# A mixture-of-experts layer behind cross-attention: eight full expert tiles moved into the end of the attention part, and two program blocks made one

## The reference, cut to what matters

```
x = x + xattn(layernorm(x), ctx, mask, mask, Wq, bq, Wk, bk, Wv, bv)    # x: 8 x 256 x 512
    # channels are the 256 rows: q, k, v = W (256x256) @ rows + b; 16 heads of 16 channels,
    # dot = q^T k / 4 over 512 x 512 positions, masked softmax, out = amap @ v
x = x + ffn(layernorm(x), gate_w, w1, w2)
    # the 2048 rows of 512 are tokens; logits over E = 8 experts; softmax, top 2, weights renormed
    gate_up = token @ w1[e].T          # 512 -> 2 x 352
    act     = silu(gate) * up
    out    += combine[token, e] * (act @ w2[e].T)      # 352 -> 512
```

## Time and profile before

| | us |
|---|---|
| median of 3 runs | 927.23 (927.05 to 927.42) |
| the profiled execution, its own time | 925.97 |
| its span, first to last instruction | 924.2 |
| TensorE busy | 815.2 (88%) |
| VectorE busy | 551.8 (60%) |
| GpSimd busy | 371.3 (40%) |
| ScalarE busy | 317.0 (34%) |

### The profile page before, as it was taken

One profiled execution on the slowest core, in us unless ns is written; L12 is line 12 of the kernel. 1 busy time (PEld: TensorE's weight loads), 2 busy tenths in 40 slices (PEclk: granted clock), 3 DMA queues, 4 the chain that ended last, 5 costly groups with the idle time before them and its releaser, 6 DMA issues. The chain is left out here.

```text
span 924.2 us, 12981 instructions
## 1 busy us (share of the span) xinstructions
PE 815.2 (88%) x3769; PEld 372.9 (40%) x3770; DVE 551.8 (60%) x1044; ACT 317.0 (34%) x615; POOL 371.3 (40%) x392
## 2 busy tenths in 40 slices
PE   4878899999989998999999888129999999999994
PEld 1233333333333332333333322116656666665662
DVE  5856588888878887888778762333333333333331
ACT  0014465555655655555566566000000000000000
POOL 6507255555745665665574242401211222212122
PEclk9559899999999999999999999559999999999998
DMA  7632668665865856765564422342456455453332
GB/s 213 200 82 92 200 196 243 201 206 176 270 181 157 278 185 179 222 181 181 178 200 144 128 76 85 103 148 51 98 128 153 77 146 120 109 156 68 68 68 34
DMA packets 84561, 138.26 MB, mean 150 GB/s; under 512 B 14737, under 2 KB 40657, under 8 KB 84514
## 3 DMA queue, kind: packets, MB, share of 16 engines
q1 hardware_dynamic: 68658, 108.27, 38.6%
q0 software_dynamic: 7744, 17.86, 9.9%
q10 hardware_dynamic: 8112, 11.55, 4.3%
HBM read 77.37 MB, written 59.36 MB: 148 GB/s over the span
## 5 line engine op out<-in xcount | busy, mean ns | idle before, releaser
L812 DVE TENSOR_REDUCE mx<-tile 128x2 f32<-128x1024 f32 x256 | 309.1, 1217 | 77.7 <-PE tile L1121 67.6
L703 ACT ACTIVATE pr<-sc 128x512 f32<-128x512 f32 x512 | 269.2, 601 | 213.1 <-PE sc L1108 210.5
L1121 PE MATMUL tile<-qk 97*128 97x512 bf16 x480 | 147.3, 390 | 27.2 <-DVE mx L812 16.1
L1108 PE MATMUL sc<-qk 100*128 100x512 bf16 x512 | 155.7, 385 | 10.9 <-DMA qk<-mxt 7.5
L1460 POOL DMA_INDIRECT out_dram<-y,ids x36 | 56.1, 1558 | 258.8 <-DVE ids L1381 254.8
L1148 PE MATMUL pvb<-pr,vp 128*32 128x512 f32 x1024 | 138.0, 611 | 0.0
L1440 ACT ACTIVATE sg<-gp 128x352 f32<-128x352 f32 x36 | 16.7, 463 | 266.7 <-PE gp L1481 266.7
L1513 PE MATMUL dp<-wring,at 128*128 (+1 forms) x216 | 98.8, 593 | 1.6 <-DVE at L1391 1.6
L1121 PEld LDWEIGHTS tile<-qk 97*128 97x128 bf16 x480 | 34.1, 98 | 158.4 <-DVE mx L812 74.5
L1481 PE MATMUL gp<-wring,xtile 128*128 x288 | 93.7, 469 | 1.1 <-DVE meta L1372 1.1
L1481 PE MATMUL up<-wring,xtile 128*128 x288 | 91.2, 460 | 0.0
(11 more groups left out here) (126 smaller groups left out, 777.2 us busy)
## 6 DMA issues: line engine op xcount, KB each, us to landing
qk<-stack_d SPq DMA_DIRECT2D x32, 768.0 KB
stack_d<-parts SPq DMA_DIRECT2D x32, 384.0 KB, 2.8
wring<-w_dram SPq DMA_DIRECT2D x32, 352.0 KB, 5.5
xl<-routed_d ACTq DMA_DIRECT2D x38, 257.0 KB, 2.7
stack_d<-parts SPq DMA_DIRECT2D x32, 256.0 KB, 3.0
pv_d<-ov SPq DMA_DIRECT2D x32, 256.0 KB, 4.2
xin<-x_dram SPq DMA_DIRECT2D x16, 256.0 KB, 5.3
cin<-ctxt_dram SPq DMA_DIRECT2D x8, 512.0 KB, 6.1
```

Source lines behind the costliest of these rows:

```text
L703: nc.scalar.activation(pr[s % 2][:, j, :], sc[(32 * u + 4 * s + j) % NSC][:, :], ACT.Exp, scale=SCALE).then_inc(exped.sem, 1)
L812: dve.tensor_reduce(cols, t[:, :, :], X, ALU.max, negate=True).then_inc(drained.sem, 1)
L1108: nc.tensor.matmul(sc[(32 * u + 4 * s + j) % NSC][:, :], ks[half(u)][0:ALL_ROWS, h, c * P:c * P + P], qs[half(u)][0:ALL_ROWS, h, :], start ...
L1121: last = nc.tensor.matmul(t[:, i, :], qs[half(w)][0:RAW_ROWS, h, c * P:c * P + P], ks[half(w)][0:RAW_ROWS, h, :], start=True, stop=True)
```

## The change

The second block goes away: its tensors become views of the attention's buffers (`xl` in `cin`, `xtl` and `sg` in `xh`, `ac` and `acT` in `qkf`, `y` in `xin`) and its PSUM banks the banks of the attention. From turn 15 (`TAIL`) on:

- TensorE counts the rows of units 0 to 12 after step 2 of turn 15 (`count_early`); VectorE's `plan_early` (a copy and 22 instructions) stands in turn 15 between `token_normalize` and `reciprocals`. It gives eight (`EARLY`) tiles that are full by these counts, taken from experts 0, 1 and 2 in this order.
- Sync loads the rows of tiles 0 and 1 (`first_rows`) in turn 15, between `store_recip` and `store_product(15, 0)`. TensorE transposes tile 0's rows in step 5, after `logits`.
- Turns 16 to 18 are written out. TensorE's `gate(0, 0)` stands ahead of the last product of unit 15, and the routing steps of units 14 and 15 stand between the steps of tiles 1 to 5. The other engines have the same mixture. The counts of all units are summed in tile 5 (`count_all`).
- The plan for the rest leaves out the eight tiles' rows: `plan_rows` (13 instructions and a copy) stands in VectorE's tile 5, `plan_experts` (13) in its tile 6. Sync issues the eight pads after the first two instructions of `plan_rows`. ScalarE loads tile 8 when the rows are planned, all rows scattered and the pads landed; the loop over pairs starts with tile 8.
- All PSUM tiles from turn 15's count on use slot 0, so each waits for the one before. Four small memsets are added at the start.

```
+NT = 52
+EARLY = 8
+TAIL = UNITS - 1
+EARLY_PLANNED, PADS_PLANNED, ROWS_PLANNED, ALL_PLANNED = 22, 24, 36, 49
```

Sync in turn 15, behind `store_recip`:

```
+                if u == TAIL:
+                    sp.wait_ge(ready.sem, ready.at(u - 1, "v"))
+                    sp.wait_ge(routed.sem, routed.at(u, 1))
+                    sp.wait_ge(padded, 16 * 5)
+                    sp.wait_ge(plan_made, EARLY_PLANNED)
+                    first_rows(0)
+                    first_rows(1)
...
+            def first_rows(n):
+                row = entry(sp, ROWS, n, E * CAP + 3 * P)
+                sp.dma_start(xl[:, n, :], routed_d[bass.ds(row, P), :]).then_inc(xl_in[n], 16)
```

GpSimd in place of turns 16 to 18 (`add` is the indirect DMA of a tile's result):

```
+            token_rstd(UNITS)
+            scatter(UNITS)
+            pool.wait_ge(x1_kept.sem, x1_kept.at(TAIL - 1, "x"))
+            add(0, 0)
+            residual(UNITS)
+            add(1, 1)
+            scatter(UNITS + 1)
+            token_rstd(UNITS + 1)
+            add(2, 0)
+            add(3, 1)
+            scatter(UNITS + 2)
+            add(4, 0)
```

ScalarE:

```
+            product_out(TAIL, 1)
...
+            tile(0, 0)
+            tile(1, 1)
+            transposed_out(UNITS)
+            tile(2, 0)
+            gate_weight(UNITS)
+            tile(3, 1)
+            tile(4, 0)
+            transposed_out(UNITS + 1)
+            tile(5, 1)
+            gate_weight(UNITS + 1)
+            silu(6, 0)
+            act.wait_ge(plan_made, ROWS_PLANNED)
+            act.wait_ge(routed.sem, routed.total())
+            act.wait_ge(padded, 16 * (E + 5))
+            load(8, 0)
+            tile(7, 1)
```

VectorE, tiles 0, 1, 5 and 6 (2 to 4 are alike, with `choose`, `rows_of` and the statistics between):

```
+            token_stats(UNITS, 0)
+            token_stats(UNITS, 1)
+            fetch(1, 1)
+            token_normalize(UNITS, 0)
+            token_normalize(UNITS, 1)
+            multiply(0, 0)
+            note(0, 0)
+
+            finish(0, 0)
+            fetch(2, 0)
+            reciprocals(UNITS, 0)
+            reciprocals(UNITS, 1)
+            multiply(1, 1)
+            scale(0, 0)
+            note(1, 1)
...
+            for step in range(6):
+                choose(UNITS + 1, step)
+            rows_of(UNITS + 1, 0)
+            rows_of(UNITS + 1, 1)
+            finish(4, 0)
+            fetch(6, 0)
+            plan_rows()
+            multiply(5, 1)
+            scale(4, 0)
+            note(5, 1)
+
+            finish(5, 1)
+            fetch(7, 1)
+            plan_experts()
+            multiply(6, 0)
```

TensorE behind turn 15 (`expand` is the `project` of the second block):

```
+            for e in range(WRING):
+                pe.wait_ge(weights_in[e], 16 * CHUNKS)
+            off = gate(0, 0)
+            product(TAIL, 7)
+            transpose_rows(1, 1)
+            expand(0, off, up[0], I, up_done)
+
+            off = gate(1, 1)
+            transpose_act(0, 0)
+            transpose_rows(2, 0)
+            expand(1, off, up[1], I, up_done)
+            pe.wait_ge(pv_out.sem, pv_out.total())
+            down(0, 0)
+            transpose_tokens(UNITS)
+
+            off = gate(2, 0)
+            transpose_act(1, 1)
+            transpose_rows(3, 1)
+            logits(UNITS)
+            expand(0, off, up[0], I, up_done)
+            down(1, 1)
+
+            off = gate(3, 1)
+            ranks(UNITS)
+            transpose_act(2, 0)
+            transpose_rows(4, 0)
+            expand(1, off, up[1], I, up_done)
+            down(2, 0)
+
+            off = gate(4, 0)
+            transpose_act(3, 1)
+            transpose_rows(5, 1)
+            transpose_tokens(UNITS + 1)
+            expand(0, off, up[0], I, up_done)
+            down(3, 1)
+            logits(UNITS + 1)
+
+            off = gate(5, 1)
+            ranks(UNITS + 1)
+            count_all()
+            transpose_act(4, 0)
+            transpose_rows(6, 0)
+            expand(1, off, up[1], I, up_done)
+            down(4, 0)
+
+            tile(6, 0)
+            tile(7, 1)
+            pe.wait_ge(plan_made, ALL_PLANNED)
+            count = pairs(pe)
+            other_tiles(pe, tile, count)
```

More of the change, by code:

```diff
@@ L124, in tile_events @@
             ev.append((-1, "k"))
+        if n == TAIL and s == 2:
+            ev.append((n, "early"))
+        if n == LAST - 1 and s == 7:
+            ev.append((n, "count"))
     return ev
@@ L275, in attention @@
         ones_made = sem("ones_made")
-        plan = sem("plan")
         padded = sem("padded")
+        plan_made = sem("plan_made")
+        passed = sem("passed")
+        experts_in = sem("experts_in")
+        xl_in = [sem(f"xl_in{k}") for k in range(2)]
+        xt_ready, xt_made = sem("xt_ready"), sem("xt_made")
+        copied = sem("copied")
+        gate_done, up_done = sem("gate_done"), sem("up_done")
+        silu_done, act_done = sem("silu_done"), sem("act_done")
+        at_ready, at_made = sem("at_ready"), sem("at_made")
+        down_done, y_made, y_added, noted = sem("down_done"), sem("y_made"), sem("y_added"), sem("noted")
         def of(ahead, *names):
@@ L335, in attention, with entry, pairs, last_tile @@
         CONST = 16 * len(const)
-        MADE = 6
+        MADE = 10
+        def entry(eng, row, n, top):
+            return eng.value_load(tab[0:1, row, bass.ds(n, 1)], min_val=0, max_val=top)
+        def pairs(eng):
+            return eng.value_load(pairi[0:1, 1:2], min_val=TOKENS // P,
+                                  max_val=(2 * TOKENS // P + E + EARLY) // 2)
+        def last_tile(eng):
+            return eng.value_load(pairi[0:1, 2:3], min_val=2 * TOKENS // P - 1, max_val=NT - 1)
+        def other_tiles(eng, tile, count):
+            with eng.Fori(EARLY // 2, count) as i:
+                tile(i * 2, 0)
+                tile(i * 2 + 1, 1)
+        def later(n, back):
+            return not isinstance(n, int) or n >= back
         def heads_in(eng, heads):
@@ L652, in _, with add @@
             part(-1, 0)
-            for u in range(LAST + 1):
+            def add(n, k):
+                pool.wait_ge(y_made, n + 1)
+                pool.wait_ge(noted, (n + 1) * 2)
+                if later(n, 1):
+                    pool.wait_ge(y_added, n * 16)
+                pool.sem_inc(passed, 1)
+                pool.indirect_dma_start(out, bass.IndirectOffsetOnAxis(ap=ids[:, k, :], axis=0),
+                                        y[:, k, :], None, compute_op=ALU.add).then_inc(y_added, 16)
+            for u in range(UNITS):
                 if has(u + 2):
@@ L719, in _, with load, silu, tile @@
             act.wait_ge(const_made, MADE)
-            for u in range(FIRST, LAST + 1):
+            for u in range(UNITS):
                 unit(u)
+            product_out(TAIL, 1)
+            def load(n, k):
+                act.wait_ge(xt_made, n - 1)
+                row = entry(act, ROWS, n, E * CAP + 3 * P)
+                act.dma_start(xl[:, k, :], routed_d[bass.ds(row, P), :]).then_inc(xl_in[k], 16)
+            def silu(n, k):
+                act.wait_ge(gate_done, n + 1)
+                if later(n, 2):
+                    act.wait_ge(act_done, n - 1)
+                nc.scalar.activation(sg[:, k, :], gp[k][:, 0:I], ACT.Silu).then_inc(silu_done, 1)
+            def tile(n, k):
+                load(n + 2, k)
+                silu(n, k)
+            tile(0, 0)
[14 more added lines that the diff above has]
+            tile(7, 1)
+            act.wait_ge(plan_made, ALL_PLANNED)
+            count = pairs(act)
+            other_tiles(act, tile, count)
+            for k in range(2):
+                act.wait_ge(xl_in[k], (count + 1) * 16)
+            act.sem_inc(passed, 1)
         @block.vector
@@ L952, in unit @@
                 split_maxima(u)
+                if u == TAIL:
+                    fetch(0, 0)
                 maximum(u, 2)
@@ L958, in unit @@
                 projection_out(u, 1)
[L960 to L975, removed]
+            planned = [0]
@@ new lines, in plan_rows @@
+            def plan_rows():
+                t = tile_of(LAST - 1, "count")
+                dve.tensor_copy(f[:, T0, :], t[0:1, 0, 0:E]).then_inc(drained.sem, 1)
+                dve.wait_ge(drained.sem, drained.at(LAST - 1, "count"))
+                do(dve.tensor_tensor(f[:, NTF, :], f[:, T0, :], io[0:1, 16:24], ALU.add))
+                do(dve.tensor_copy(padrow[:, :], f[:, NTF, :]))
+                assert planned[0] == PADS_PLANNED
+                do(dve.tensor_scalar(fi[:, 0, :], f[:, T0, :], float(P - 1), None, ALU.add))
@@ L985, in plan_tiles @@
[L985 to L991, removed]
@@ L1012, in key_parts, with tile @@
+            def tile(n, k):
+                finish(n - 1, 1 - k)
+                fetch(n + 1, 1 - k)
+                multiply(n, k)
+                scale(n - 1, 1 - k)
+                note(n, k)
             def key_parts(u):
@@ L1076, in _ @@
             normalize(-1)
-            for u in range(LAST + 1):
+            for u in range(UNITS):
                 unit(u)
[L1079 to L1082, removed]
+            token_stats(UNITS, 0)
[12 more added lines that the diff above has]
+            note(1, 1)
+            finish(1, 1)
+            fetch(3, 1)
```

(70 more changed lines are left out.)

396 lines of the change are left out of this document (190 added, 206 removed).

## The result

| | before | after |
|---|---|---|
| median, us | 927.33 (927.05 to 928.64, 4 runs) | 895.86 (893.08 to 897.02, 4 runs) |
| ratio | | 0.9652 (95% interval 0.9625 to 0.9679) |
| profiled execution, span | 925.97, 924.2 | 895.12, 893.3 |

The change saves 31.5 us of the medians and 30.9 us of the two profiled spans. The forecast was 888.6, a gain of 38.6: the direction and the mechanism held, and 7 to 8 us of the gain are missing. The measured 895.9 lies in the stated range of 883 to 902, but outside the forecast's own 884 to 893 and inside rival A's 894 to 901. The hole is gone from the strip: the page after has no slice under 8 in the middle of the PE row, where the earlier trace rows has a 1 and a 2.

The account below looks back on a forecast made before the run. TensorE bounds the kernel, with a 45.5 us hole: gate(8) moves from 682.49 to 641.9 (40.6 us), less 1 for clock and 1 for handoffs, 38.6; 925.97 becomes 887.4, plus 1.3 for the median: 888.6 us, range 883 to 902.

Parts of the forecast that it names:

- rival A: Tail: the chain of units 14 and 15 or the pads come late, giving back 5 to 12 us: 894 to 901; chance 0.16.
- What bounds: TensorE has a hole of 45.5 us (572.5 to 618.0), working 7.48 us; behind it, it is the bound without a gap.
- Eight full tiles: Experts 0 to 2: early row counts give eight full tiles together; no padding tile is added and 28 tiles stay.
- Rival D: Early plan: fewer than eight full tiles, each missing one run on padding and costing 8.1 us more; chance 0.03.
- Turn 15: Early plan takes 5.2 us; TensorE waits for tile 0's rows, step 6 starts 2.1 us late, gate(0) at 573.6.
- The eight tiles and what lies between: Tile 0 takes 6.2 us, tiles 1 to 7 56.6, routing steps between them 4.2; gate(8) could start at 640.6.
- The pads: Before tile 8: the last pad lands at 633.4, tile 8's rows at 636.5; TensorE stalls 1.3 us (0 to 6).
- The pads' neighbours: Pads, alone in the old hole, now meet a tile's row load, unit 15's scatter and an add; no cost taken.
- The sentence on DMAs that share 16 engines: Skill text: queues of Sync, ScalarE and GpSimd share 16 engines, so pads land later; estimated 1 us, not taken.
- The clock: The 1.7 us pause in turn 15's step 5 could slow TensorE's clock: 0 to 2.7 us, 1 taken.
- Rivals B and C: Eight tiles: B, two to three at half clock, about 905, chance 0.07; C, all eight, 953, 0.04 with other losses.
- What comes behind it is the same code in the same order: From gate(8) to the end, 28 tiles and the tail keep the old 241.7 us.

Follow-up runs that it names:

- ctl: The changed kernel run once more with no edit: 895.1 us (890.97 to 897.82, 6 runs), ratio 0.9648 to the kernel before.

## Why the prediction was right, and where it was short

- *What bounds:* right. TensorE was the bound behind the hole, and filling the hole moved the end by what gate(8) moved: 682.33 to 648.81 is 33.5 us.
- *Eight full tiles:* right. 36 tiles in all, 28 behind gate(8), in the same 233.7 us. Rival D is out.
- *Turn 15:* right. The plan's 23 instructions took 4.9 us (560.96 to 565.87; 5.2 taken), the rows held TensorE 1.2 us (1.7 expected), and gate(0) came 23.8 us behind the turn's start (24.1 expected; 24.9 to 26.1 in the four other executions, by the clock). The turn itself began 2.8 us late by chance.
- *The eight tiles and what lies between:* right to 0.2 us. Gate(0) to gate(7) took 58.7 us in all seven executions; the terms of the forecast give 58.9. The chain of units 14 and 15 was hidden, as said: x1 of unit 14 came at 577.7 (576 expected), of unit 15 at 598.1 (597).
- *The pads:* **this is the step that failed, by its size.** A stall of 1.3 us was taken, 0 to 6 allowed; it was 4.3 to 4.7. From the first pad to tile 8's rows 14.5 us were taken (622.0 to 636.5) and 17.7 measured (624.3 to 642.0): 3.2 more, the whole difference. Of these 0.9 are in Sync's issuing (9.3 from the first pad to the last, 8.4 taken; the eight in a row took 9.65 to 9.98 us in all seven executions, 8.63 in the kernel before), 1.0 in the landing of the last pad, 0.5 in ScalarE's read of the row number and 0.8 in the load. This is rival A in one of its forms; its other form, a late chain of units 14 and 15, did not come, and the drain is no part of it.
- *The pads' neighbours:* misread. The prediction has the pads alone in the old hole, and lets them meet a row load, the scatter of unit 15 and an add. The scatter was there before: issued at 600.30 and 601.73, with the first pad at 600.41; here it is 624.30 and 625.72, with the first pad at 624.31. And no row load is issued between 613.96 and 638.46. New are the adds, issued at 628.98 among the pads and at 636.61 ahead of tile 8's load. From 626 to 628 the DMA engines move 338 GB/s at a busy share of 0.91, from 630 to 632, with the add under way, 155 GB/s at 1.00. That points at the adds, but no run took them away, so it is not shown; and why Sync's issuing takes longer stays open. The sentence on DMAs that share 16 engines, set aside with its 1 us, pointed to the right place, with too little.
- *The clock:* half right. The pause in step 5 cost nothing beyond itself in the first profile (clock 1.00 behind it), but 1.2 to 2.2 us in the four others; 1 was taken, 0 to 2.7 allowed. The pause at tile 8 cost 1.5 to 3.2 us behind it, and no term tied the clock to that stall. Rivals B and C are out: over the eight tiles it was 1.00.
- *"What comes behind it is the same code in the same order":* wrong at the very end. One block in place of two carries the drain of the attention's 32 indirect DMAs to the end of the program, 2.6 us. The forecast had no term for it.

The sum, by the means of the stages in the executions whose edit leaves them alone, against the terms of the forecast: 25.1 us for 24.1 up to gate(0), 58.7 for 58.9 up to gate(7), 14.7 for 9.4 (8.1 and the stall of 1.3) up to gate(8), and 2.6 more at the end. That is 8.7 us more; 2 of them were allowed, 1 for the clock and 1 for handoffs, for which the rows show no cost. 38.6 - 6.7 = 31.9, and the medians give 31.5. The first profile's 30.9 hold a start that was 2.8 us late by chance, and the clock at its mild end both in turn 15 and at tile 8. That the two nearly cancel is luck.

## What to carry to other kernels

Work moved in front of a late chain is worth the hole that it fills, and its own length can be forecast to a fraction of a us from steady rows; what can't is the transfer that ends the filled stretch, since its old duration was taken beside other traffic than it meets now. Look up in the trace what stood beside it, price it with its new neighbours, and wait only for the part that the next step reads. Count a wait of TensorE with the slow matmuls behind it: the one of 1.2 us in turn 15 cost up to 3.6. And when blocks are merged, ask what each block's end did for free.

## What the runs showed of the hardware

- A drain of GpSimd costs some 0.083 us for each indirect DMA issued since the last drain (2.35 us for 28, 2.69 for 32, 2.99 for 36, 5.63 for 68), with all of them landed. Each of these DMAs is issued for 128 rows; whether the price goes by the DMA or by the row was not tried. A drain in a place with slack takes this off the end (0.05 us left), at the cost of waiting there for what is in flight.
- A pause of TensorE of 4.3 to 4.7 us brought its granted clock to 0.5 (1.2 GHz) for the next matmuls (0.50 from 642.3 to 646.0 in ctl): up took 3.24 us in the chain of one execution, for 2.37, and 4.90 in the timeline of another, for 2.53. The Trainium skill says, in "TensorE: Matmul & The Clock Gate", section "What's actually happening", that the number of slow matmuls differs from run to run of the same kernel; these two agree.
- A pause of 1.1 to 1.3 us in turn 15, with TensorE at 1.00 before it, was followed by 0.50 in four executions (over stretches of 2 to 4 us, by which turn 15 came to cost 1.2 to 2.2 us more) and by 1.00 in the fifth.
